# Four early tiles mixed on fourths, and the second half's weight sums by one VectorE instruction, in a two-layer ternary and NF4 feed-forward kernel

## The reference

```python
def _L0_ffn_ref(x, w, b):                 # ternary weights
    scale = mean(abs(w), axis=0)          # one number for each output column
    ternary = where(abs(w) < 0.05, 0.0, sign(w)) * scale
    return x @ ternary + b
def _L1_ffn_ref(x, q_weight, q_scale, bias, lora_A, lora_B):
    w = NF4_LEVELS[q_weight].reshape(-1, 64) * q_scale[:, None]
    base = einsum("bsi,oi->bso", x, w) + bias
    return base + 4.0 * ((x @ lora_A.T) @ lora_B.T)
x = x + _L0_ffn_ref(einsum("bct,bcd->bdt", x, W0[token]), ...)
x = x + _L1_ffn_ref(einsum("bct,bcd->bdt", x, W1[token]), ...)
```

## Time and profile before

| | us |
|---|---|
| median of 3 runs | 343.64 (343.38 to 344.93) |
| the profiled execution's own time | 344.56 |
| its span in the trace | 342.5 |

### The profile page before, as it was taken

The page is one execution under the profiler, slowest core; times in us unless marked ns, Lnnn a source line. Parts: engine busy times, 40 slices in busy tenths (PEclk is TensorE's granted clock), DMA queues, the critical chain, the costliest instruction groups (busy, mean ns, idle before and its releaser), DMA issues.

```text
span 342.5 us, 8187 instructions
## 1 busy us (share of the span) xinstructions
PE 332.4 (97%) x3142; PEld 271.4 (79%) x3142; DVE 236.0 (69%) x356; ACT 164.5 (48%) x300; POOL 245.0 (72%) x160
## 2 busy tenths in 40 slices
PE   7999999989999999999799999999999999999996
PEld 6868778778888778887678888888888888888884
DVE  7787567899999999999999736346263462624623
ACT  1799357877897787788171403214032140411400
POOL 0298999998896896986578966766467664677642
PEclk9999999999999999999999999999999999999999
DMA  6894511644354245300100151412513124150302
GB/s 229 291 341 132 201 33 33 271 168 159 118 167 162 93 157 177 141 10 13 55 2 3 65 189 63 150 44 74 181 65 131 63 84 169 67 169 23 124 31 92
DMA packets 25800, 40.60 MB, mean 119 GB/s; under 512 B 7810, under 2 KB 16002, under 8 KB 25762
## 3 DMA queue, kind: packets, MB, share of 16 engines
q1 hardware_dynamic: 25090, 39.48, 33.3%
q10 hardware_dynamic: 672, 0.61, 0.5%
HBM read 25.40 MB, written 14.68 MB: 117 GB/s over the span
## 4 chain that ended last, share of the span: by engine, by line
PE 51%; DVE 20%; POOL 12%; issue 8%; ACT 4%; DMA 1%; SPq 1%; DVEq 0%; POOLq 0%; ACTq 0%
PE acc L1268 45%; POOL col_scale L631 4%; DVE hl L914 3%; DVE ys L941 3%; POOL x_first L604 3%; PE spare L1154 2%; PE xT L1154 2%; POOL x_first L611 2%; DVE side_n L953 2%; ACT spare L762 2%; DVE W L988 2%; DMA w_in<-in_L_ffn_w 1%; POOL side_p L638 1%; DVE side_p L953 1%; DVE side_n L956 1%
## 5 line engine op out<-in xcount | busy, mean ns | idle before, releaser
L1268 PE MATMUL acc<-W,hh 128*128 128x512 f32 x256 | 81.4, 389 | 0.0
L1228 PE MATMUL acc<-T,hh 128*128 128x512 f32 x192 | 76.5, 398 | 0.0
L1228 PE MATMUL acc<-T,hl 128*128 128x512 f32 x192 | 75.0, 391 | 0.0
L604 POOL TENSOR_TENSOR X<-X,bias 128x1024 f32<-128x1024 f32 x28 | 68.1, 2432 | 0.0
L762 ACT ACTIVATE spare<-q_raw 128x512 f32<-128x512 int32 x96 | 56.1, 599 | 20.2 <-DVE side_n L953 5.0
L1040 DVE TENSOR_TENSOR X<-X,acc 128x512 f32<-128x512 f32 x48 | 32.9, 685 | 36.7 <-PE acc L1268 28.9
L1268 PEld LDWEIGHTS acc<-W,hh 128*128 128x128 f32 x256 | 48.0, 188 | 10.0
L663 POOL TENSOR_TENSOR X<-X,ys 128x512 f32<-128x512 f32 x24 | 30.5, 1299 | 34.1 <-DVE ys L1029 34.1
L1268 PE MATMUL acc<-W,hl 128*128 128x512 f32 x128 | 49.8, 389 | 0.0
L797 ACT ACTIVATE hh<-xT 128x512 fp32r<-128x512 f32 x16 | 8.7, 595 | 77.6 <-PE xT L1154 77.6
L1228 PEld LDWEIGHTS acc<-T,hh 128*128 128x128 f32 x192 | 36.0, 188 | 8.0
(11 more groups left out here) (98 smaller groups left out, 606.5 us busy)
## 6 DMA issues: line engine op xcount, KB each, us to landing
out<-X SPq DMA_DIRECT2D x22, 512.0 KB, 3.1
X<-in_x SPq DMA_DIRECT2D x12, 512.0 KB, 3.4
X<-out SPq DMA_DIRECT2D x12, 512.0 KB, 3.8
q_raw<-in_L_ffn_q_weight SPq DMA_DIRECT2D x16, 256.0 KB, 2.9
w_in<-in_L_ffn_w SPq DMA_DIRECT2D x14, 256.0 KB, 6.8
x_first<-in_x SPq DMA_DIRECT2D x4, 512.0 KB, 5.1
out<-x_first SPq DMA_DIRECT2D x4, 512.0 KB, 4.6
out<-X SPq DMA_DIRECT2D x4, 256.0 KB, 2.0
```

The lines of the kernel that those rows point to most:

```text
L604: pool.tensor_tensor(x_of(g), x_of(g), bias[:, :], ALU.add).then_inc(s_xb, 1)
L1228: mm = pe.matmul(acc[:, bank_of(q), :], a[:, k, :], T0[:, n, k, :], start=(k == 0 and j == 0), stop=(k == KB - 1 and j == 1))
L1268: mm = pe.matmul(acc[:, bank, :], a[:, k, :], w1(part, c, k), start=(k == 0 and j == 0), stop=(k == HB - 1 and j == len(terms) - 1))
```

## The change

**Order and form of the first four tiles.** `mixed` is gone, `mixed_batches` serves all tiles of the first layer; `high_x` and `low_x` follow. Tile 1 goes to another place in `acc`. `first` gets free block ranges, and PE now runs a few blocks of several tiles in turn. Products of no use (`idle`) stand before `turn_b` (seven instead of five), before tile 0 (four) and before tile 1 (two). ACT copies half of the turned `lora_B`. POOL issues the first two weight loads and the matrices of tiles 2 and 3, which SP and ACT issued. On DVE the low parts of tiles 1 and 2 stand earlier among the ternary steps.

**Sums.** POOL keeps the seven additions of the first half. The second half's eight blocks are added by one `tensor_reduce` on DVE, behind `leave_y(2)`, which goes ahead of the `loraA` subtraction; `column_sums(1)` waits for it and stands one group of eight products later, `column_sums(0)` stands behind part of tile 3.

**Shares.** The weights of the steps are 5 (eight steps), 10 (eighteen) and 6 (three); piece `d` is turned not before step 8 + `d`; `colscale(1)` stands at `g == 2` of ACT's loop.

```diff
-    WARM = 5
+    WARM = 7
...
+    SHARES = [5] * (NH * F) + [10] * 18 + [6] * 3
     def share(total, m):
-        m = min(m, NH * NT - 3)
-        whole = 3 * NH * F + 10 * (NH * (NT - F) - 3)
-        return total * (3 * min(m, NH * F) + 10 * max(0, m - NH * F)) // whole
+        return total * sum(SHARES[:m]) // sum(SHARES)
...
     def turned_in(d):
-        return max(NH * F, ready_in(d) + 2)
+        return max(NH * F + d, ready_in(d) + 2)
...
         def batch(g, s):
+            if g == 1:
+                return acc[:, 2 + s, :].rearrange("p (k c) -> p k c", k=KB)
             return xT[:, s, :, :].rearrange("p b c -> p (b c)").rearrange("p (k c) -> p k c", k=KB)
...
             load_condition(sp, 1, 0)
+            load_weights(sp, 2, 0)
             load_x(2)
-            load_condition(sp, 2, 0)
-            load_weights(sp, 1, 0)
             load_weights(sp, 3, 0)
-            load_condition(sp, 3, 0)
             load_weights(sp, 4, 0)
+            load_weights(sp, 5, 0)
             load_x(3)
-            load_condition(sp, 3, 1)
-            load_weights(sp, 5, 0)
...
-                    if d > 3 and ready_in(d - 3) // NH == g or d == 3 and g == F:
+                    if max(F, ready_in(d - 3) // NH) == g:
                         load_q(d)
...
-            sums(0, 1, KB)
-            sums(1, 1, KB)
+            load_weights(pool, 0, 0)
+            load_weights(pool, 1, 0)
+            pool.wait_ge(s_tok, 16)
+            pool.wait_ge(s_fill, 1)
+            for g in (2, 3):
+                for s in range(2):
+                    load_condition(pool, g, s)
+            sums()
             add_bias(0)
             result_half(0)
             add_bias(1)
             result_half(1)
+            add_bias(2)
             pool.wait_ge(s_scales, 16)
-            add_bias(2)
+            add_bias(3)
             result_half(2)
             for m in range(NH * F - 3):
                 weights_of(m)
-            add_bias(3)
...
             load_condition(act, 0, 1)
-            load_weights(act, 0, 0)
             load_condition(act, 1, 1)
-            load_weights(act, 2, 0)
-            load_condition(act, 2, 1)
+            act.wait_ge(s_bT, 2)
+            act.activation(lora_columns(1), lora_turned(1), ACT.Copy).then_inc(s_loraB, 1)
             high_x(0, 0)
             high_x(0, 1)
             signs(0, 2)
             absolute(0, 2)
+            high_x(1, 0)
+            high_x(1, 1)
             signs(0, 3)
             absolute(0, 3)
-            high_x(1, 0)
-            high_x(1, 1)
...
             for g in range(SB):
-                if g == 1:
+                if g == 2:
                     colscale(1)
...
             ternary(0, 1)
+            low_x(1, 0)
+            low_x(1, 1)
             ternary(0, 2)
             ternary(0, 3)
-            low_x(1, 0)
-            low_x(1, 1)
+            low_x(2, 0)
+            low_x(2, 1)
             ternary(0, 4)
-            low_x(2, 0)
             ternary(0, 5)
-            low_x(2, 1)
...
                 ternary(1, k)
+            leave_y(2)
+            dve.wait_ge(s_abs, NH * KB)
+            dve.tensor_reduce(col_scale[:, BANK:T], w_in[:, :, BANK:T].rearrange("p k f -> p f k"),
+                              mybir.AxisListType.X, ALU.add).then_inc(s_reduce, 1)
             dve.wait_ge(s_ah, 1)
             dve.tensor_tensor(loraA[64:P, :], a_raw[64:P, :], loraA[64:P, :].bitcast(F32),
                               ALU.subtract).then_inc(s_al, 1)
-            leave_y(2)
...
             def column_sums(n):
-                pe.wait_ge(s_sum, (n + 1) * (KB - 1))
+                if n == 0:
+                    pe.wait_ge(s_sum, KB - 1)
+                else:
+                    pe.wait_ge(s_reduce, 1)
                 pe.wait_ge(s_fill, 3)
-                pe.wait_ge(s_hl, NH * 3)
+                pe.wait_ge(s_hl, NH * F)
...
+            idle(WARM)
             turn_b()
-            mixed(0)
-            mixed(1)
-            mixed(2)
-            first(0, 0, 0)
-            first(1, 0, 0)
-            mixed(3)
-            first(0, 0, 1)
-            first(1, 0, 1)
+            idle(4)
+            mixed_batches(0)
+            idle(2)
+            mixed_batches(1)
+            first(0, 0, 0, 2)
+            first(1, 0, 0, 2)
+            mixed_batches(2)
+            first(0, 0, 2, 4)
+            first(1, 0, 2, 4)
+            first(2, 0, 0, 4)
+            first(0, 0, 4, 6)
+            mixed_batches(3)
+            first(1, 0, 4, 6)
+            first(2, 0, 4, 6)
+            first(0, 0, 6, KB)
+            first(1, 0, 6, KB)
+            first(2, 0, 6, KB)
+            first(3, 0, 0, HB)
             column_sums(0)
-            first(2, 0, 0)
-            first(2, 0, 1)
-            first(3, 0, 0)
-            first(3, 0, 1)
-            first(0, 1, 0)
-            first(0, 1, 1)
-            first(1, 1, 0)
+            first(3, 0, HB, KB)
+            first(0, 1, 0, HB)
+            first(1, 1, 0, HB)
+            first(0, 1, HB, KB)
+            first(1, 1, HB, KB)
             column_sums(1)
-            first(1, 1, 1)
-            first(2, 1, 0)
-            first(2, 1, 1)
+            first(2, 1, 0, KB)
             mixed_batches(F)
-            first(3, 1, 0)
-            first(3, 1, 1)
+            first(3, 1, 0, KB)
```

More of the change, by code:

```diff
@@ L366, in build @@
         s_mix = [sem(f"s_mix{k}") for k in range(NM)]
+        s_mix_early = {g: sem(f"s_mix_early{g}") for g in (2, 3)}
         s_b0 = sem("s_b0")
@@ L397, in build @@
         s_sum = sem("s_sum")
+        s_reduce = sem("s_reduce")
         s_colsum = sem("s_colsum")
@@ L716, in high_x @@
                 act.wait_ge(s_xT, NH * g + h + 1)
-                if g >= F:
-                    if h == 0:
-                        act.wait_ge(s_acc, F + g - 3 if g < F + 2 else NH * (g - 1))
-                    act.activation(high(g)[:, :, h * C:(h + 1) * C], batch(g, h), ACT.Copy
-                                   ).then_inc(s_hh, 1)
-                    return
-                act.activation(high(g)[:, h * HB:(h + 1) * HB, :], turned(g, h), ACT.Copy
+                if g >= F and h == 0:
+                    act.wait_ge(s_acc, F + g - 3 if g < F + 2 else NH * (g - 1))
+                act.activation(high(g)[:, :, h * C:(h + 1) * C], batch(g, h), ACT.Copy
                                ).then_inc(s_hh, 1)
@@ L1131, in _ @@
         def _(pe):
-            def mixed(g):
-                pe.wait_ge(s_mix[g % NM], 32 * (g // NM + 1))
-                arrived(pe, g)
-                if g == 2 or g == 3:
-                    pe.wait_ge(s_hl, NH * (g - 1))
-                for k in range(KB):
-                    mm = pe.matmul(turned(g, k // HB)[:, k % HB, :], x_of(g)[:, k * P:(k + 1) * P],
-                                   mix[:, g % NM, :], start=True, stop=True)
-                    if k % HB == HB - 1:
-                        mm.then_inc(s_xT, 1)
             def quarters(g, turn):
@@ L1201, in mixed_pair, with first @@
                 quarters(v, 1).then_inc(s_xT, NH)
-            def first(g, n, h):
+            def first(g, n, start, stop):
                 q = n * F + g
-                if h == 0:
+                if start == 0:
                     bank_free(pe, q)
                     if q < NH:
-                        pe.wait_ge(s_loraB, q + 1)
-                    if g == 2:
-                        pe.wait_ge(s_hl, NH * F)
-                pe.wait_ge(s_hl, NH * g + h + 1)
-                for k in range(h * HB, (h + 1) * HB):
+                        pe.wait_ge(s_loraB, NH)
+                    pe.wait_ge(s_hl, NH * max(g + 1, 2 if q in (2, 3) else 0))
+                for k in range(start, stop):
                     pe.wait_ge(s_T0, n * KB + k + 1)
```

62 lines of the change are left out of this document (32 added, 30 removed).

## The result

The changed kernel takes 351.29 us (median of 4 runs, 350.51 to 353.88); the kernel before, run beside it, 343.80. The ratio is 1.0219, 95% interval 1.0166 to 1.0271: 7.5 us slower. The forecast was 348.1, 4.5 slower, with a range up to 350.5: the direction was right, the size 3 us too small, and the time lies 0.8 us above the range. The profiled execution took 351.12 us with a span of 349.5; before it was 344.56 with 342.5.

The account below looks back on a forecast made before the run. DVE decides when PE's second layer begins. Main loop at 60.1 plus PE's 115.2 gives 175.3 against 170.78, 4.5 us later: 344.56 + 4.5 = 349.1, as a median 348.1; range 342.3 to 350.5.

Parts of the forecast that it names:

- rival 3: PE at half spacing after its wait before tile 5's mix: 3.6 us more, 351.7; chance 0.05.
- a distance to a median: Last step of the sum: profiled execution lay 0.9 above its kernel's median, 343.64, so 349.1 became 348.1.
- a shift of that point is a shift of the end: Behind the second layer's start at 170.78, PE has no idle time that the change touches.
- the 1.86 us before 164.82: PE's longest wait for DVE, late in the main loop, goes: last steps hold fewer maxima, piece 14 turns earlier.
- the four waits of ACT: First half: the new order makes ACT wait 1.0, 1.1, 0.7 and 1.25 us; last absolute ends at 33.7.
- Up to 2 us of lateness there would be hidden: Start: late loads of the first two weight pieces and x would be hidden behind tile 0.
- the ends of 4.4 and 8.9: DVE's reduction over 4096 values: bounds of 4.4 us from plain operations and 8.9 from a spaced copy; 8.6 taken.
- Hidden by the next wait: A slower PE clock behind `column_sums(1)` would be hidden by the next wait.
- Rival 1: The reduction runs at the pace of values in a row, 4.4 us: 343.9, no change; chance 0.24.
- Rival 2: First half's early lead survives, ACT does not wait, last ternary step before 31.5, reduction under 5: 340.3; chance 0.14.
- Rival 4: The fourths do not overlap because early tiles find PE slow; tile 0 at 10.7, 2 us later: 350.1; chance 0.05.

Follow-up runs that it names:

- x4: The kernel before with only the second half's sums changed to the reduction on DVE, right behind the last ternary step: 345.37 us, ratio 1.0037.
- x5: The changed kernel with the shares and steps of turning of the kernel before: 348.00 us, ratio 1.0094.
- x6: The kernel before with only the change's first half (mixing on fourths, loads by POOL, product order): 346.85 us, ratio 1.0080.
- x8: The kernel before with the second half's sums as plain DVE additions between ternary steps, and earlier second column sums: 350.06 us, ratio 1.0151.
- x9: As x8 on the kernel before, but the running sum lies in PSUM and only the last addition writes SBUF: 342.49 us, ratio 0.9940.
- x15: x9 plus only the end of the new shares, the last three steps holding 6 instead of 10 parts: 343.41 us, ratio 0.9968.
- x10: The changed kernel with the first two weight pieces loaded by ACT's queue again instead of by POOL: 351.78 us, ratio 1.0216.
- x2: The changed kernel with the reduction summing eight neighbouring values instead of eight lying 4 KB apart: 348.99 us, ratio 1.0119.
- x3: The changed kernel with extra unread products on PE in three places where it waits: 350.36 us, ratio 1.0184.
- x11: The changed kernel with x10's weight loads on ACT's queue and extra unread products in PE's three waits: 350.12 us, ratio 1.0160.
- x13: The changed kernel with the first column sums behind 44 of the first half's products instead of 56: 350.78 us, ratio 1.0206.
- x1: The changed kernel with the second half's sums as seven POOL additions again, no reduction on DVE: 351.98 us, ratio 1.0232.
- x14: x13 plus extra products filling all of PE's waits, early gaps included: 348.95 us, ratio 1.0124.

## Why the prediction was too low, step by step

**The step that failed.** The path was right: what stands on VectorE behind the reduction delays the main loop on PE, and PE's delay at the end of the loop comes out. Three terms of the sum were wrong. It took tile 5's mix and the loop's first products at full pace, 1.1 us for the mix, right behind a wait that it put at 3.7 us itself, and left the slower clock to rival 3, outside the range; the mix took 1.98, the loop began 1.2 us later than forecast (0.8 of it the mix) and took 0.4 more. It took a shift of the second layer's start for a shift of the end; 0.8 us came on top behind that point. And it took 0.9 us off for a distance to a median.

**What bounds the kernel.** Right to the start of the second layer. Wrong behind it: "a shift of that point is a shift of the end" leaves out 0.8 us. PE waits 0.72 there for a `ys` of VectorE. Every run with the end of the new shares has a wait of 0.7 to 0.8 at this place (all but x4, x5, x6, x8 and x9); x15, which has nothing else of the shares, has it too. The prediction let the 1.86 us before 164.82 go, which came true, and did not ask what VectorE does next.

**The first half.** Three of the four waits of ACT came as worked out: 0.79, 1.03 and 1.19 for 1.0, 1.1 and 1.25; the fourth was 0.95 for 0.7. Missing were two arrivals: tile 0's mix ended at 9.4 instead of 8.7, behind a wait of 1.57 us for its matrix, and a sign step waited 0.55 for its weights. "Up to 2 us of lateness there would be hidden" spoke of weights and x; the matrix, which came late, was not asked about, and that POOL's queue made it late would have been wrong as well (x10). ACT's own work took 21.1 us instead of 20.6. So the last absolute ended at 35.1, not 33.7.

**The reduction.** 7.28 us, between the ends of 4.4 and 8.9 and 1.3 below the value taken. It began 1.4 later than forecast (36.32 for 34.95), so its end, 43.60, met the 43.55 on record: two errors that cancel, which is luck. PE's wait for it was 4.71 us for 6.4, since PE too came later (38.95 for 37.1). The lower end of the bound was right too, as x2 showed: 4.41 in a row. The Trainium skill (Advanced Engine Details and Errata, SBUF Cachelines) says that a new line at each access costs; the reduction and x2 agree with it for reads. The plain pace in the Trainium skill (VectorE: DVE Perf Modes, The perf-mode tier table), with no word on distance, agrees with x2 alone.

**The chain behind it.** `colscale(1)` at 50.32 for 50.6, low parts of tile 4 done at 59.24 for 59.1 (the terms on record add up to 59.3, so the forecast was 0.2 us low by a slip). Then the mix took 1.98 for 1.1 and the loop began at 61.30 for 60.1; its first products were slow too (0.60, 0.42 and 0.38 apart instead of 0.23), and the loop took 115.63 us for 115.2. That is rival 3, which I had given 0.05: its mechanism was there, at 1.4 us (0.8 in the mix, 0.6 in the first products) instead of 3.6. x3 shows the cause, and the fill of x3 and x11 is worth 0.7 to 1.9 us at the end. It should have been a term of the sum, since the sum itself contained the waits of 6.4 and 3.7 us. "Hidden by the next wait" for the first of them was right (products end at 50.98, `colscale(1)` at 50.90; in x3, with fast products, VectorE waits 1.25 us there all the same).

**The sum.** Against the profiled execution: 344.56 + 4.5 + 1.2 (start of the loop) + 0.4 (in it) + 0.8 (behind it) = 351.5; measured 351.12. The last step took 0.9 off, because the profiled execution of before lay that far above the median of three runs. In the later series that median was 344.0 to 344.5, near the 344.56 of the profiled execution. The changed kernel's profiled execution lay 0.2 below its median. That subtraction is the last 0.9 of the 3 us.

**The rivals.** Rival 1 said that a reduction at the pace in a row would be no change at all, 343.9. At that pace (x2) the kernel was still 1.19% slower. Its saving was sized fairly (4.2 us for 4.2 us of reduction; measured 2.3 to 3.4 for 2.87), its starting point was not. Rival 2 needed a last ternary step before 31.5; it ended at 35.8. Rival 4 did not occur as described: tile 0 was late by a transfer, and the slow tile seen in x10 and x13 was tile 2.

**What the prediction did not see** is where the price lies. It told the story around the reduction; alone, that costs 1.3 us (x4), because it fills holes that VectorE had, and undoing it gains nothing (x1). The new shares cost 3.0 to 4.3 us and the first half 2.4 to 3.3. The six further maxima that the shares put ahead of tile 4's low parts stood in the sum, but no rival asked what the kernel does without them.

## What to carry to other kernels

Price an operation that is moved to another engine by the holes it fills there: alone, a reduction of 7.5 us cost 1.3. Test each part of a change both alone and undone: here the reduction looked like the cause, yet undoing it gained nothing, while the shares cost in all four pairs. Where a sum puts several microseconds of waiting on TensorE, price the slower clock that can follow them, in the sum or at least in the range. A forecast of a median from one profiled execution should not subtract that execution's distance from a median of three.

## What the runs showed of the hardware

- A reduction on VectorE over 4096 values took 7.28 us with the values 4 KB apart and 4.41 with neighbours (the changed kernel, x2).
- An addition on VectorE with two SBUF operands took 0.68 us with POOL idle and 2.31 beside a bias addition of POOL, which itself took 2.98 instead of 2.41; with one operand in PSUM it took 0.69. The Trainium skill (SBUF — State Buffer, Who interferes with whom) says that a VectorE instruction with two SBUF inputs contends with a GpSimd instruction that reads SBUF; these rows agree.
- The granted clock fell to a mean of 0.66 in 40 to 50 us of the changed kernel, behind a wait of PE of 4.71 us (0.50, which is 1.2 GHz, from 43 to 48 us), and to 0.83 in 10 to 20 us of x13 with gaps of only 0.35 to 0.57 us; with the gaps filled (x3, x14) both were 1.00. It does not fall each time: in the changed kernel the same early gaps left it at 1.00, and behind a wait of 3.23 us tile 5's mix took 1.98 us there and 1.16, at 1.00, in x10.
